# Attention and routed experts on one core: zero fills spread over the attention rounds, gate logits in four column groups, bias adds and weight splits placed elsewhere

## What is computed

```
x = x + attention(layernorm(x))          # softmax(Q K^T / 4) V, then Wo, bo
xf = layernorm(x)
gate_logits = xf @ gate_w.T              # 2048 x 8
top_vals, top_idx = top_k(gate_logits, 2)
w = softmax(top_vals)
y_all = einsum('td,eod->teo', xf, expert_w) + expert_b
out = x + sum over the two experts of w * y_all[t, top_idx]
```

## Times and profile before

| what | us |
|---|---|
| three runs | 1881.07, 1886.57, 1893.58 |
| median of them | 1886.57 |
| the profiled execution | 1873.43 |
| its span, first to last instruction | 1871.7 |
| PE busy | 1672.0 (89%) |
| DVE busy | 1428.8 (76%) |
| ACT busy | 1245.8 (67%) |
| POOL busy | 469.3 (25%) |

### The profile page before, as it was taken

The page is one execution under the profiler, slowest core; times in us unless marked ns, Lnnn a source line. Parts: engine busy times, 40 slices in busy tenths (PEclk is TensorE's granted clock), DMA queues, the critical chain, the costliest instruction groups (busy, mean ns, idle before and its releaser), DMA issues.

```text
span 1871.7 us, 38031 instructions
## 1 busy us (share of the span) xinstructions
PE 1672.0 (89%) x13750; PEld 803.3 (43%) x13751; DVE 1428.8 (76%) x1461; ACT 1245.8 (67%) x2287; POOL 469.3 (25%) x699
## 2 busy tenths in 40 slices
PE   5899908999999999999999999999999998559970
PEld 3533303444444444444444444444444456317860
DVE  3297807999999999999999999999999526542214
ACT  2324706888888888888888888888888873303320
POOL 3111122232222223222222322222232351060016
PEclk9996958999999999999999999999999999669995
DMA  6337322122223112212311122221112232054547
GB/s 195 84 107 158 109 101 56 28 47 56 35 37 67 28 28 47 56 36 40 63 28 30 29 55 39 32 50 27 29 30 60 106 90 81 1 193 139 167 136 250
DMA packets 74538, 138.14 MB, mean 74 GB/s; under 512 B 19320, under 2 KB 23432, under 8 KB 73648
## 3 DMA queue, kind: packets, MB, share of 16 engines
q1 hardware_dynamic: 46352, 80.25, 17.9%
q0 software_dynamic: 25616, 54.21, 10.2%
q10 hardware_dynamic: 2448, 1.84, 0.6%
HBM read 82.61 MB, written 52.17 MB: 72 GB/s over the span
## 4 chain that ended last, share of the span: by engine, by line
PE 82%; DMA 7%; issue 4%; DVE 2%; POOL 2%; ACT 1%; ACTq 1%; another core or an unknown queue 0%; SPq 0%; POOLq 0%; DVEq 0%
PE bank L789 30%; PE bank L750 22%; PE bank L779 14%; PE bank L870 8%; DMA slots_x<-be_sb 6%; PE bank L722 3%; PE bank L953 1%; PE bank L931 1%; POOL ys L438 1%; POOL xs L438 1%; PE bank L892 1%; PE bank L737 1%; DVE max_kc L1039 1%; DMA q_st<-q_parts 0%
## 5 line engine op out<-in xcount | busy, mean ns | idle before, releaser
L1039 DVE TENSOR_REDUCE max_kc<-bank 128x1 f32<-128x1024 f32 x1024 | 1240.9, 1222 | 74.3 <-PE bank L750 50.7
L627 ACT ACTIVATE arena_p<-bank 128x512 f32<-128x512 f32 x2048 | 1109.0, 596 | 246.5 <-PE bank L779 217.9
L789 PE MATMUL bank<-arena_p,v_cur 128*32 128x256 f32 x8192 | 661.3, 395 | 5.7 <-issue 5.7
L750 PE MATMUL bank<-k_st,q_st 48*128 48x512 f32 x2048 | 514.9, 501 | 64.2 <-DVE max_kc L1039 58.9
L779 PE MATMUL bank<-q_st,k_st 50*128 50x512 f32 x2048 | 451.1, 411 | 0.3 <-ACT arena_p L627 0.3
L750 PEld LDWEIGHTS bank<-k_st,q_st 48*128 48x128 f32 x2048 | 192.5, 185 | 494.1 <-issue 381.2
L779 PEld LDWEIGHTS bank<-q_st,k_st 50*128 50x128 f32 x2048 | 298.4, 187 | 36.4 <-ACT arena_p L627 22.2
L789 PEld LDWEIGHTS bank<-arena_p,v_cur 128*32 128x32 f32 x8192 | 163.2, 108 | 297.3 <-issue 154.9
L378 POOL DMA_DIRECT2D sums<-o_acc x128 | 63.9, 506 | 265.6 <-ACT o_acc L617 265.4
L381 POOL DMA_DIRECT2D sums_rec<-sums x32 | 18.5, 577 | 427.8 <-DVE sums L1070 427.8
L1160 DVE TENSOR_TENSOR x2T_lo<-bank,x2T_hi 128x512 fp32r<-128x512 f32 x39 | 27.0, 692 | 96.7 <-ACT x2T_hi L633 96.7
(11 more groups left out here) (146 smaller groups left out, 942.4 us busy)
## 6 DMA issues: line engine op xcount, KB each, us to landing
q_st<-q_parts SPq DMA_DIRECT2D x192, 128.0 KB, 4.7
slots_x<-be_sb POOLq DMA_DIRECT2D x39, 256.0 KB, 2.3
xs<-slots_x SPq DMA_DIRECT2D x39, 256.0 KB, 2.7
slots_y<-ys SPq DMA_DIRECT2D x39, 256.0 KB, 2.0
q_parts<-parts SPq DMA_DIRECT2D x16, 512.0 KB, 3.0
we_raw<-in_L_ffn_expert_w POOLq DMA_DIRECT2D x8, 1024.0 KB, 5.9
at_parts<-o_hl POOLq DMA_DIRECT2D x128, 64.0 KB, 2.3
k_st<-k_parts SPq DMA_DIRECT2D x48, 128.0 KB, 4.8
```

Of the source, the lines that this page charges most:

```text
L627: act.activation(probs[:, u % PRING, :], bank[:, ring_bank(("score", u)), :], ACT.Exp, scale=SCALE).then_inc(p_ready, 1)
L750: return pe.matmul(bank[:, 2 + 2 * (m % 2) + q, :], q_st[r:r + CROW, j % SLOTS, h, qt * P:(qt + 1) * P], k_st[r:r + CROW, j // NC % KSLOTS ...
L789: mm = pe.matmul(bank[32 * h:32 * h + 32, 6, half], v_cur[:, kt, :], probs[:, (REP * kt + h) % PRING, half], start=(kt == 0 and part == 0) ...
L1039: dve.reduce_max(max_kc[:, m:m + 1], bank[:, 2 + 2 * (m % 2):4 + 2 * (m % 2), :].rearrange("p a s -> p (a s)"), AX.X).then_inc(m_done, 1)
```

## The change

- The 39 zero fills move from their place between projections and rounds into the rounds: after `divide_outputs(i)` (and the expert's load, where there is one) POOL issues fills 2(i-1) and 2(i-1)+1, waiting before each for the one before it. Rounds 1 to 19 have two and round 20 one; after that one POOL waits for it and loads `expert_b`.
- The gate logits: `wg_sb` is widened from 8 to 32 columns with zeros. The four products of a tile are no longer accumulated: each goes to its own 32 partitions of bank 6. ACT copies 128 partitions instead of 8, and the transpose back becomes a product with `quarters`, a 128 x 8 matrix that adds the four partial sums.
- On POOL, the last bias adds `add_bias_o(NC - 1)` move ahead of `divide_outputs(N)`.
- Weight splits: ACT makes the fifth and sixth high part at n = 13 and 14 instead of both at 13, and the seventh and eighth after the logits instead of one at n = 17 and one after them. DVE makes the fifth low part at n = 14, and the sixth to eighth in the bias loop at tiles 3, 7 and 11; before, the fifth to seventh stood at n = 15, 16 and 17, and the eighth in the bias loop at tile 7.
- At the start DVE has one memset (128 x 128) and one reduction (128 x 128) more.

```diff
-        wg_sb = sb("wg_sb", [P, KD, E])
+        wg_sb = sb("wg_sb", [P, KD, 32])
...
-        EA = 7
+        EA = 6
...
-        lgT = o_acc[0:E, :]
+
+        lgT = o_acc
+        quarters = gates[:, 4:8, :].rearrange("p n e -> p (n e)")
...
-            pool.wait_ge(consts, 4)
-            for z in range(NS):
-                pool.dma_start(slots_x[z * P:(z + 1) * P, :], be_sb[:, :]).then_inc(zero_dma, 16)
-
-                pool.wait_ge(zero_dma, 16 * (z + 1))
-            pool.dma_start(be_sb[0:E, :], expert_b).then_inc(wc_dma, 16)
             pool.dma_start(bo_sb[:, :], bo.partition_broadcast(P)).then_inc(wc_dma, 16)
-            pool.dma_start(wg_sb[:, :, :], gate_w.rearrange("(k p) n -> p k n", p=P)).then_inc(wc_dma, 16)
+            pool.wait_ge(consts, 6)
+            pool.dma_start(wg_sb[:, :, 0:E], gate_w.rearrange("(k p) n -> p k n", p=P)).then_inc(wc_dma, 16)
...
                 if i % NC == 0:
                     load_expert(i // NC)
+                for z in range(2 * (i - 1), min(2 * i, NS)):
+                    if z > 0:
+                        pool.wait_ge(zero_dma, 16 * z)
+                    pool.dma_start(slots_x[z * P:(z + 1) * P, :], be_sb[:, :]).then_inc(zero_dma, 16)
+                if 2 * (i - 1) < NS <= 2 * i:
+                    pool.wait_ge(zero_dma, 16 * NS)
+                    pool.dma_start(be_sb[0:E, :], expert_b).then_inc(wc_dma, 16)
...
             residual(NC - 1)
+            add_bias_o(NC - 1)
             divide_outputs(N)
-            add_bias_o(NC - 1)
...
-                act.activation(lgT[:, :], bank[0:E, 6, :], ACT.Copy).then_inc(lgT_ready, 1)
+                act.activation(lgT[:, :], bank[:, 6, :], ACT.Copy).then_inc(lgT_ready, 1)
...
-                if n == 13:
+                if n in (13, 14):
                     act.wait_ge(wo_full, TT * (NC - 1))
-                    expert_hi(ORDER[4])
-                    expert_hi(ORDER[5])
-                if n == 17:
-                    act.wait_ge(wo_full, NKT)
-                    expert_hi(ORDER[6])
+                    expert_hi(ORDER[n - 9])
...
-                    mm = pe.matmul(bank[0:E, 6, t * P:(t + 1) * P], wg_sb[:, d, :], xgT[:, g % 2, d, :],
-                                   start=(d == 0), stop=(d == KD - 1))
+                    mm = pe.matmul(bank[32 * d:32 * d + 32, 6, t * P:(t + 1) * P], wg_sb[:, d, :], xgT[:, g % 2, d, :],
+                                   start=True, stop=True)
...
-                    mm = pe.transpose(bank[:, 7, n * E:(n + 1) * E], lgT[:, t * P:(t + 1) * P], ident[0:E, 0:E])
+                    mm = pe.matmul(bank[:, 7, n * E:(n + 1) * E], lgT[:, t * P:(t + 1) * P], quarters[:, 0:E],
+                                   start=True, stop=True)
...
-                if n >= NKT - 1:
-                    expert_lo(4 + n - (NKT - 1))
+                if n == 14:
+                    expert_lo(4)
...
-                if n % 4 == 3:
-                    if n == 7:
-                        expert_lo(EA)
+                if n % 4 == 3 and 5 + n // 4 < E:
+                    expert_lo(5 + n // 4)
```

## The result

| | median, us | lowest to highest | profiled execution |
|---|---|---|---|
| before, four runs beside it | 1883.82 | 1875.1 to 1893.58 | 1873.43 |
| changed, four runs | 1803.37 | 1797.72 to 1806.26 | 1806.26 |

The ratio is 0.957, with an interval from 0.951 to 0.962: 80 us less, where 66 were forecast. Yet the profiled executions differ by 67.2 us, almost the sum of 66.3. Both facts have to be explained: the gain in the medians, which is larger than the sum, and the agreement of the two profiles with it.

A forecast was written before the change was run, and what follows sets the result against it. PE was taken as the bound, busy 89% of the span, with 58.5 us idle behind POOL's fills. Terms -60.2 + 0 + 2 - 7.8 - 3.3 + 3 = -66.3 us from the median 1886.57 gave 1820 us, range 1803 to 1838.

The forecast's parts named there:

- the sum: All terms over the whole kernel added together: -66.3 us.
- Minus 60.2 us: First round: PE's 58.5 us idle time behind POOL's serial fills, and 1.7 us of slow restart, go.
- I keep the median's figure: Whole kernel: forecast taken from the median 1886.57, giving 1820 us, not from the profiled 1873.43, giving 1807.
- slower fills: Possible source of the 13 us between profiled execution and median; they would go too, which the range holds.
- The first rival: Early rounds: the half clock from about 157.5 us, put to the fills' traffic, goes too: 14 us, 1806; chance 0.12.
- The moved fills: Two fills per round fit POOL's idle time before the copy to `v_cur`: 0 us, worst 0 to 3.
- The last adds: Gate stage: bias adds ahead of the last division delay the first transposes 7 to 8 us; net plus 2 us.
- the collision: Gate stage: third `xg` took 5.47 us instead of 0.55 during POOL's adds; 4.9 us on the chain goes.
- Logits: Gate stage: four column groups make a tile's logits 0.33 us, 0.8 at the half clock; together minus 7.8 us.
- Splits: Gate stage: moving the high and low weight parts removes waits of 2.3 and 1.0 us: minus 3.3 us.
- low parts in the bias loop: Bias loop: two low parts now stand there, 4.6 us at worst; plus 3 us, from 0 to 4.6.
- the bias loop set the end: Bias stage: the scatter's first tile could be transposed about 3 us before the bias loop let PE do so.

The follow-up runs named there:

- e1: Kernel before with only the zero fills spread into the rounds, logits, adds and splits as before: 1796.0 us, ratio 0.957.
- b1: Kernel before, nothing changed, profiled again: 1880.04 us in one execution.
- b3: Kernel before, nothing changed, profiled a third further time: 1879.80 us in one execution.
- e11: Kernel before with the fills spread and the moved weight splits, adds and logits as before: 1793.6 us, ratio 0.956.
- e12: Kernel before with all 39 fills in their old place but issued without waiting for each: 1814.0 us, ratio 0.966.
- b2: Kernel before, nothing changed, profiled a second further time: 1879.63 us in one execution.
- a0: Changed kernel itself, unaltered, run again on a second chip as yardstick: 1801.9 us, ratio 0.962.
- e4: Changed kernel with the last bias adds back behind the last output's division: 1794.2 us, ratio 0.957.
- e9: Kernel before with the fills spread and the logits in four column groups, adds and splits as before: 1795.2 us, ratio 0.956.
- e10: Kernel before with fills spread, logits in column groups, and last adds between the sums' collection and the reciprocals' store, splits as before: 1793.9 us, ratio 0.957.
- e13: Changed kernel with last adds inside the last division and only the eighth low part in the bias loop: 1786.8 us, ratio 0.954.
- e3: Changed kernel with the 39 fills back in their old place ahead of the rounds: 1876.5 us, ratio 1.001.
- e7: Changed kernel with the last adds inside the last division, between the sums' collection and the reciprocals' store: 1791.1 us, ratio 0.956.
- e6: Changed kernel with the sixth to eighth low parts behind the bias loop's last tile: 1803.5 us, ratio 0.963.

## Why the prediction was off, step by step

**The step that failed: "Minus 60.2 us" for the wait, and with it "I keep the median's figure".** The cause was right: the wait hangs on the fills' chain and goes with it. The size was wrong. The term was read from one execution and is 60.2; moving the fills alone gave 79 us in the medians (e1). PE's loss up to the end of the restart is the early half clock times 0.42, the wait, and the half clock behind it times 0.42. In the execution shown that is 14 + 58.5 + 1.7 = 74.5 us; in b1 to b3 it is 85, 86 and 88, as their waits are 3 to 15 us longer and their restarts cost 8 to 12 us instead of 1.7. Of this a kernel with spread fills keeps only its own early half clock, 10 to 34 us in the profiles, which is 4 to 14 us. So the term lay between 60 and 84 us, and the sum took its lowest value: the shortest wait and restart, with the longest early half clock kept. From b3's rounds' end to e1's it is 82 us; from that of the profile shown to the changed kernel's, with 24 us of early half clock, it is 63. That is why the two profiles agree with the sum, and it is luck of the two executions.

The 13 us between profile and median were kept as if they lay elsewhere. They are not the same thing as the missing 19, though: on the chip of e1 the kernel before had a median of 1875.3, 2 us above the profiled execution, and the gain there was 79 us all the same. Against the profiled execution's own time the sum gave 1807; the timed runs gave 1803.4, and 1801.9 on the second chip, which is close because two errors offset each other: the wait was put too low, and the edits behind the rounds, put down at -6.1, came to about 0. The prediction allowed only for slower fills; those are 2 to 3 us, and the restart is the larger part. How much of it the timed executions have stays open, as b1 to b3 took 1880 where the median beside them was 1872.

**The wait's two ends.** Its end hangs on the fills' chain. Its beginning hangs on PE, which in the profile shown was late by 0.42 x 34 = 14 us from its early half clock; a late PE waits less. With spread fills the early half clock counts directly, and the rounds end between 1457.6 and 1468.5 in the profiles. So the gain is no single number; the medians have it at 79.

**The first rival (the early half clock goes as well) fell.** It put the stretch down to the fills' traffic. The measured time lies near its 1806, and inside the range only because the range's lower end was put there for it: that is luck, not this mechanism. e11, with no fill before 230 us, has it in full:

```profile
170.00:180.00 10.00, 10.00 (x60) 3.11 (x58) 6.05 (x5) 5.28 (x10) 0.00 (x0) 0.50 0.80 121
180.00:190.00 10.00, 10.00 (x56) 3.38 (x60) 5.73 (x6) 4.71 (x10) 0.00 (x0) 0.50 0.92 118
190.00:200.00 10.00, 10.00 (x93) 3.99 (x85) 8.96 (x10) 7.73 (x15) 0.00 (x0) 0.97 0.02 6
```

while e12, with every fill there, has 10 us, and so has b1, whose fills stand as in the kernel before. By the rule of the Trainium skill's page TensorE: Matmul & The Clock Gate, section What's actually happening, a busy engine regains its clock; here it does, but after times between 10 and 34 us, and one kernel unchanged had both 10 (b1, b2) and 34 (before, b3).

**The moved fills: right, 0.** PE waits for none of them.

**The last adds: sign right, +2 against 6.5 to 8 in the gate stage (a0 and the changed profile beside e4).** The delay was forecast 7 to 8 us and is 9.3 at PE (20.3 behind the rounds' end instead of 11.1). The 4.9 us that the collision was to give back hardly came: with the adds behind, e4's collision took 3.35 us and its gate stage was 6.5 to 8 us shorter.

**Logits: -7.8 against -4.8 to -8.4 (e9).** The forecast had the last four tiles at the half clock on both sides, and there it is -6.8 to -8.4; beside e1, whose clock came back, it is -4.8. The prices were right: 0.36 a tile for 0.33, 0.65 at the half clock for 0.8, the block back 0.81 to 0.96 for 0.8. The last block back takes 1.88 us at the half clock, where 0.6 more than the old block was put down; it was 0.59, so 1.3 more. The estimate that the prediction worked out from the Trainium skill's page TensorE: Matmul & The Clock Gate, section Measured speedup vs the span model, 0.32 to 0.41 us, holds this case's 0.36.

**Splits: -3.3 against -4.2 to -6.1 (e9 to e4, e11); low parts in the bias loop: +3 against +2.1 to 3.3, for another reason.** I had the bias loop set the end, from the earlier trace rows, where PE's first expert transposes wait 0.94 us. That too was an unusual execution: in b1 to b3 they wait 9.6 to 10.0 us for `xs<-slots_x`, so the scatter sets it. In the changed kernel's profile the three issues are 2.07 + 1.06 + 1.05 = 4.2 us longer than the usual 0.97; one such issue the kernel before had too in b1 to b3. The rule of the Trainium skill's page SBUF — State Buffer, section SBUF: two separate sides, which I had set aside, agrees with nearly all of these traces: one stretched issue where one low part stands in the bias loop (e9, e10, e13 and others), three for three in the changed kernel, a0 and e3, two for three in e4, e7 and e11, and none in e6. The earlier trace rows had no issue over 1.214 us with one low part in its midst, from which I took that there was no such cost; the same low part in b1 to b3 stretched one issue to 2.76, 3.04 and 2.82 us.

**Together** these parts were to give -6.1. Logits and splits together give -9.0 in the gate stage beside e1 (e4), and more beside executions at the half clock, the low parts +2.1 to 3.3 and the adds +6.5 to 8. Beside e1 that is about 0: by the stages a0 is 0.6 us below e1, by the medians 6 above, on another chip. Over all profiles of either code, gate and bias together are 151.2 to 152.9 us (changed, a0, e3) against 151.7 to 158.2 (before, b1 to b3, e1, e2, e12). e3 has the whole at 0 within 4 us. So the gain is the fills', and the edits behind the rounds cancel within a few microseconds.

## What to carry to other kernels

A wait in one profile is not its worth: ask what sets its two ends, look for time that the waiting engine lost just before and just behind it, and take two or three executions before a wait is priced or a difference between profile and median is put aside. Spread long serial transfers over an engine's idle places. Put POOL's arithmetic into its waits for its own transfers (here between `sums` and its reciprocals), not ahead of a transfer for which others wait, and price a DVE operation beside indirect transfers by the issues it stretches.

## What the runs showed that was not expected

- With PE busy throughout, the half clock lasted 10 to 34 us behind a pause of about 1 us near 155 us, and 4 to 28 us behind pauses of 8 to 74 us, in no order of the pauses' length. A microsecond at the half clock loses 0.42 here (steps of 2.16 us, 204.31 to 206.47 in e12, against 1.26).
- The same four adds on POOL stretched one `xg` on DVE to 5.45 to 5.47 us in every profile with the old logits and the adds behind, and to 3.34 and 3.35 in the two with the logits in groups (e9, e4). Why is not shown.
- In the profile before and in e6, single waits of DVE in the bias loop took 4 to 5 us; in b1 and e1 the longest is 2.9. The 65.0 us of the bias stage in the profile before go with them. The cause stays open, as does what sets the length of the half clock.
